# A perceiver block on one core: ScalarE takes over one layer's normalisation, and the projections behind it change their order

## The chip, the cores and the metric

The kernel runs on one core of one Trainium2 chip. The metric is the device time of one execution in microseconds (us), as the median of three runs of the kernel before.

## The reference

Inputs are `x` (8 batches of 128 rows, 512 wide) and a context (8 batches of 2048 rows, 384 wide). Three residual layers follow one another:

```
x = x + cross_attention(layernorm(x), context)   # 8 heads of 64, softmax over the 2048 context rows, then @ Wo + bo
n = layernorm(x)
x = x + n + read(n)                              # q, k, v = n @ W + b; causal logits q k^T per batch;
                                                 # softmax over the QUERY axis, / sqrt(512), times v
x = x + ffn(layernorm(x))                        # 512 -> 2048 -> 512, relu, values rounded to small float formats
```

`layernorm` subtracts the row mean and divides by sqrt(variance + 1e-5).

## The kernel before, in words

One program holds an instruction list for each engine, written out by hand; engines meet on counted semaphores alone, and each engine takes its own list strictly in the order written. A float32 operand of a large product is split into a high and a low f16 part, and `three_passes` (line 370) makes high*high + low*high + high*low: 12 matmuls of 128x512 for one projection tile.

**The long first part** (to about 750 us of the span) is the cross attention: 128 slots of `steady(s)` on every engine. TensorE works several slots behind in its later steps, so a tail of five more calls of `steady` (slots SLOTS to SLOTS+4) follows it.

**The seam** is what this change touches. It leads from the cross attention to the second layer:
- TensorE (lines 606 to 625) makes the output projections `project_out(r)` of the eight 128-row groups r, the first seven between the last calls of `steady`. Then come `turn(1, r)`, four float32 transposes of group r of the normalised rows `o_all` into one of two PSUM banks (`v_ps`, `k_ps`, alternating), and `project(i)`, the q, k and v products of the second layer. They go into four banks `t_bank` (`e_ps`). Products 0 to 11 read rows of groups 0 to 3 (the first half), products 12 to 23 the second half; before, each half has its four q tiles first, then k, then v.
- ScalarE (lines 857 to 871) writes the high part of each transposed group (`turned_high`, line 824) and empties the q and k banks (`q_or_k`, line 830).
- VectorE (from line 1122) adds each projection to `x` (`residual`, line 1050), takes the row moments (`row_moments`, lines 1037 to 1042), normalises (`norm`, line 1044, reads `xr`, writes `o_all`), writes the low part of each transposed group (`turned_low`, line 1030) and empties the v banks (`v_rows`, line 1059). In the tail it also still accumulates the cross attention (`accumulate`, line 952).
- GpSimd (from line 1272) adds the bias row to `x` (`add_bias`), finishes the last stages of the cross attention (`p_low`, `o_norm`), and turns each variance into 1/sqrt (`inverse_deviation`, lines 1262 to 1265, which calls `inverse_root`: one addition at line 1200, one power at line 1202). Its order there is: add_bias 0, p_low, add_bias 1, p_low, o_norm, add_bias 2, inverse_deviation 0, then add_bias 3, 4, 5 each followed by inverse_deviation 1, 2, 3, then o_norm of the last stage, add_bias 6, inverse_deviation 4, add_bias 7, inverse_deviation 5, 6, 7, and then `add_norm` of all eight groups (line 1267).
- SyncE issues the transposing DMAs that feed `project_out`, the last pair after the last `o_norm`; ScalarE issued the loads of `xr` and of the weights earlier.

The order of TensorE at the seam, before, is this (lines 610 to 619):

```
turn(1, 0)
turn(1, 1)
turn(1, 2)
turn(1, 3)
project_out(7)
for i in range(4):
    turn(1, 4 + i)
    project(i)
for i in range(4, 13):
    project(i)
```

`turn(1, 2)` and every later one waits until VectorE has taken the low part of the group two before (`tr_split`), because the two PSUM banks alternate. A `project` of the first half waits for the low parts of groups 0 to 3.

**Behind the seam** come the per-batch logits, softmax and reads of the second layer, woven into the products of the second half, and then the feed-forward layer, which TensorE also fills.

Of the kernel before, what the change touches and what calls it, by code (L numbers as in the profile page):

```python
# [4 lines left out]
F32 = mybir.dt.float32  # L5
# [7 lines left out]
P = 128  # L13
# [41 lines left out]
def perceiver_kernel(nc, x, ctx_t, xwq, xwk, xwv, xwo, xbo, awq, abq, awk, abk, awv, abv,  # L55
# [11 lines left out]
        ("o_f", [P, 2, DH], F32),  # L67
# [56 lines left out]
     q_max, bias, low, fade, acc, o_rec, o_sum, o_f) = keep.values()  # L124
# [23 lines left out]
    with ExitStack() as ctx:  # L148
# [78 lines left out]
        ln_step = sem("ln_step")  # L227
        xn2_ready = sem("xn2_ready")
# [56 lines left out]
        def turn_at(what, r):  # L285
            return turns.index((what, r))

# [81 lines left out]
        def _(pe):  # L369
# [136 lines left out]
            def turn(what, r):  # L506

                at = turn_at(what, r)
                pe.wait_ge(xn2_ready, at + 1)
# [31 lines left out]
            def project(i):  # L541

                half, what, t = i // 12, i % 12 // 4, i % 4
                pe.wait_ge(wx_split, 4 * what + 8)
                pe.wait_ge(tr_split, turn_at(1, 4 * half + 3) + 1)

                if i < 4:
                    pe.wait_ge(x1_ready, (3, 4, 7, 8)[i])
                else:
                    copied_a, copied_v = 8 * ((i - 4) // 12) + min((i - 4) % 12 + 1, 8), 4 * ((i - 4) // 12) + (i - 4) % 12 - 7  # L550
                    if (i - 4) % 12 < 8:
                        pe.wait_ge(mm2_copied_a, copied_a)
                    else:
                        pe.wait_ge(mm2_copied_v, copied_v)
                acc = t_bank[i % 4]
# [55 lines left out]
            turn(1, 1)  # L611
            turn(1, 2)
            turn(1, 3)
            project_out(7)
            for i in range(4):
                turn(1, 4 + i)
                project(i)
            for i in range(4, 13):
                project(i)
# [42 lines left out]
        def _(act):  # L662
# [166 lines left out]

            def q_or_k(i):  # L830
                half, what, t = i // 12, i % 12 // 4, i % 4
                act.wait_ge(mm2_filled, i + 1)
                dst, col = ((q2, bq_col), (k2, bk_col))[what]
                act.activation(dst[:, t, half * 512:half * 512 + 512], t_bank[i % 4], ACT.Identity,
                               bias=col[:, t:t + 1], scale=1.0 / W_SCALE).then_inc(mm2_copied_a, 1)
# [21 lines left out]
            for r in range(5):  # L857
                turned_high(1, r)
            act.wait_ge(small_landed, 96)
            for i in range(4):  # L860
                q_or_k(i)
                if i < 3:
                    turned_high(1, 5 + i)
            for i in range(4, 8):
                q_or_k(i)
# [21 lines left out]
        def _(dve):  # L887
# [156 lines left out]
            def norm(i):  # L1044
                r = i % B
                dve.wait_ge(rstd_ready, len(x_groups) + i + 1)
# [12 lines left out]
            def v_rows(i):  # L1059
                half, t = i // 12, i % 4  # L1060
# [62 lines left out]
            for s in range(SLOTS + 1, SLOTS + PV_LAG + 1):  # L1123
                steady(s)
                residual(s - SLOTS - 1)
                if s > SLOTS + 1:
                    norm(s - SLOTS - 2)
            residual(5)
            norm(4)
            turned_low(1, 0)  # L1130
            turned_low(1, 1)
            residual(6)
            norm(5)
            turned_low(1, 2)
            norm(6)
            turned_low(1, 3)
            turned_low(1, 4)
            residual(7)
            norm(7)
            for r in range(5, B):  # L1140
                turned_low(1, r)
            dve.wait_ge(small_landed, 96)

# [3 lines left out]
            for i in range(8, 12):  # L1147
                v_rows(i)
                w1_high(0, i - 8)
            for b in range(4):  # L1150
                mask_logits(b)
                prob_norm(b)
                if b >= 1:
                    add_read(b - 1)
                    norm(B + b - 1)
            add_read(3)
            norm(B + 3)
# [6 lines left out]
            for b in range(5, B):  # L1164
# [4 lines left out]
                norm(B + b - 1)  # L1169
            add_read(7)  # L1170
            norm(B + 7)
# [13 lines left out]
        def _(pool):  # L1185
# [76 lines left out]
            def inverse_deviation(i):  # L1262
                r = i % B
                pool.wait_ge(var_ready, i + 1)
                inverse_root(mean_var[:, r, 1:2], rstd[:, r:r + 1], exponent[:, 0:1], len(x_groups) + i)

            def add_norm(r):

                pool.wait_ge(xn2_ready, r + 1)
# [55 lines left out]
```

## Time and profile before

| what | us |
|---|---|
| median of 3 runs | 982.43 |
| lowest and highest run | 982.3, 982.64 |
| the profiled execution, its own time | 983.69 |
| its span in the trace | 981.9 |
| TensorE (matmul) busy | 949.6 |
| VectorE, ScalarE, GpSimd busy | 565.5, 583.7, 463.9 |

The span is the part of the execution that the trace covers; the execution's own time has 1.8 us around it. Times within the trace count from the start of the span. In the rows, PE is TensorE's matmuls, PEld its weight loads, DVE is VectorE, ACT ScalarE, POOL GpSimd, and PEclk is the granted clock of TensorE as a share of 2.4 GHz.

### The profile page before, as it was taken

The numbers are of one execution on the slowest core, as the hardware profiler recorded it, in microseconds if no ns is written. First come the engines' busy times: TensorE is split into PE (matmuls) and PEld (weight loads), VectorE is DVE, ScalarE is ACT, GpSimd is POOL, SyncE is SP. The second block draws the span as 40 slices with busy tenths as digits, with TensorE's granted clock in tenths as the row PEclk, the third lists the DMA queues.
The fourth block names the chain that finished last, engine by engine and source line by source line (L and its number), as shares of the span: only waits on it lengthen the run. The fifth ranks groups of instructions, "written<-read, shape, count | busy, mean of one in ns | idle before, by whom it ended". The sixth has DMA issues, their size and how long they took to land.

```text
span 981.9 us, 19435 instructions
## 1 busy us (share of the span) xinstructions
PE 949.6 (97%) x7437; PEld 579.3 (59%) x7440; DVE 565.5 (58%) x1016; ACT 583.7 (59%) x1095; POOL 463.9 (47%) x355
## 2 busy tenths in 40 slices
PE   4789999999999999999999999999999899999998
PEld 2356666666666666666666666666665445544443
DVE  6535656565656565555555555557777735565533
ACT  3357777777777777777777777776666121222220
POOL 3245555666555556665555566655456640000000
PEclk9899999999999999999999999999999899999999
DMA  8138666766777676666676668659778301013311
GB/s 289 65 87 160 136 129 130 140 130 124 137 157 133 138 141 129 130 138 126 154 141 140 130 130 135 135 95 185 160 153 172 65 1 43 1 44 97 97 33 75
DMA packets 304491, 117.95 MB, mean 120 GB/s; under 512 B 281232, under 2 KB 281232, under 8 KB 304400
## 3 DMA queue, kind: packets, MB, share of 16 engines
q1 hardware_dynamic: 289968, 88.92, 46.6%
q10 hardware_dynamic: 14432, 27.79, 9.9%
q8 instruction: 61, 1.00, 0.4%
q14 instruction: 30, 0.25, 0.1%
HBM read 45.36 MB, written 2.10 MB: 48 GB/s over the span
## 4 chain that ended last, share of the span: by engine, by line
PE 90%; DVE 4%; POOL 2%; DMA 1%; issue 1%; ACT 1%; SPq 0%; ACTq 0%; POOLq 0%; DVEq 0%
PE v_ps L375 28%; PE k_ps L375 26%; PE e_ps L375 14%; PE e_ps L416 10%; PE o_ps L436 6%; PE o_ps L439 3%; PE o_ps L603 3%; DMA wq_raw<-in_xwq 1%; PE v_ps L576 1%; DVE x_in L899 0%; DMA raw<-in_ctx_t 0%; DVE stats L1040 0%; PE k_ps L520 0%; POOL p_l L1220 0%; POOL rstd L1202 0%
## 5 line engine op out<-in xcount | busy, mean ns | idle before, releaser
L1220 POOL TENSOR_TENSOR p_l<-p_f,p_h 128x1024 f16<-128x1024 f32 x128 | 278.0, 2172 | 278.8 <-ACT p_f L744 274.0
L940 DVE TENSOR_TENSOR k_l<-k_ps,k_h 128x512 f16<-128x512 f32 x128 | 88.5, 692 | 154.7 <-ACT k_h L716 154.7
L744 ACT ACTIVATE p_f<-e_ps,bias 128x512 f32<-128x512 f32 x256 | 176.8, 691 | 0.0
L742 ACT ACTIVATE p_h<-e_ps,bias 128x512 f16<-128x512 f32 x256 | 174.6, 682 | 0.1
L945 DVE TENSOR_REDUCE q_max<-e_ps 128x2 f32<-128x1024 f32 x128 | 156.6, 1223 | 14.4
L932 DVE TENSOR_TENSOR v<-v_ps,v 128x512 f16<-128x512 f32 x128 | 88.8, 694 | 113.4 <-ACT v L708 113.3
L375 PE MATMUL v_ps<-wv_h,ctx_h 128*128 128x256 f16 x768 | 127.3, 275 | 4.7 <-DVE v L932 3.3
L375 PE MATMUL v_ps<-wv_l,ctx_h 128*128 128x256 f16 x768 | 126.4, 274 | 0.0
L375 PE MATMUL v_ps<-wv_h,ctx_l 128*128 128x256 f16 x768 | 126.1, 273 | 0.0
L1212 POOL TENSOR_TENSOR ctx_l<-raw,ctx_h 128x1536 f16<-128x1536 f32 x32 | 99.2, 3099 | 28.8 <-ACT ctx_h L697 28.8
L708 ACT ACTIVATE v<-v_ps 128x512 f16<-128x512 f32 x128 | 76.2, 595 | 51.3 <-PE v_ps L375 51.0
L436 PE MATMUL o_ps<-v,pt_h 128*128 128x130 f16 x1024 | 106.2, 220 | 0.1
L375 PE MATMUL k_ps<-ctx_h,wk_h 128*128 128x512 f16 x384 | 104.2, 380 | 0.0
L375 PE MATMUL k_ps<-ctx_h,wk_l 128*128 128x512 f16 x384 | 103.8, 379 | 0.0
L375 PE MATMUL k_ps<-ctx_l,wk_h 128*128 128x512 f16 x384 | 103.8, 379 | 0.0
L375 PEld LDWEIGHTS v_ps<-wv_h,ctx_h 128*128 128x128 f16 x768 | 64.9, 98 | 65.0 <-issue 56.8
L439 PE MATMUL o_ps<-v,pt_l 128*128 128x65 f16 x1024 | 102.8, 192 | 0.0
L436 PEld LDWEIGHTS o_ps<-v,pt_h 128*128 128x128 f16 x1024 | 91.9, 97 | 15.8 <-issue 1.0
L439 PEld LDWEIGHTS o_ps<-v,pt_l 128*128 128x128 f16 x1024 | 90.4, 98 | 14.9
L722 ACT ACTIVATE bias<-q_max 128x2 f32<-128x2 f32 x128 | 26.3, 206 | 108.8 <-DVE q_max L945 105.9
L716 ACT ACTIVATE k_h<-k_ps 128x512 f16<-128x512 f32 x128 | 76.5, 597 | 24.4 <-PE k_ps L375 23.8
L375 PEld LDWEIGHTS v_ps<-wv_l,ctx_h 128*128 128x128 f16 x768 | 75.4, 98 | 8.9
(163 smaller groups left out, 1255.3 us busy)
## 6 DMA issues: line engine op xcount, KB each, us to landing
raw<-in_ctx_t ACTq DMA_DIRECT2D x26, 768.0 KB, 5.6
w_raw<-in_w_t SPq DMA_DIRECT2D x32, 256.0 KB, 2.8
raw<-in_ctx_t SPq DMA_DIRECT2D x6, 768.0 KB, 4.7
pt_h<-p_h SPq DMA_TRANSPOSE x128, 3.2
pt_l<-p_l SPq DMA_TRANSPOSE x128, 3.4
xr<-in_x ACTq DMA_DIRECT2D x8, 256.0 KB, 3.5
out<-xr SPq DMA_DIRECT2D x8, 256.0 KB, 2.0
x_in<-in_x SPq DMA_DIRECT2D x4, 256.0 KB, 5.2
```

The costliest lines, as they stand in the source:

```text
L375: mm = pe.matmul(acc, a(c), m(c), start=(i == 0), stop=(i == len(todo) - 1))
L416: mm = pe.matmul(e_ps[s % 2][:, h, :], left[rows, p, tokens], right[rows, n % 2, cols], start=first, stop=last)
L436: pe.matmul(acc_bank[:, h * VW:h * VW + VW], pt_h[:, s % T_RING, h * JT + j, :], v[g][:, tile, 2 * (p % 2) + h, :], start=(j == 0 and h == ...
L439: mm = pe.matmul(acc_bank[:, h * VW:h * VW + DH + 1], pt_l[:, s % T_RING, h * JT + j, :], v[g][:, tile, 2 * (p % 2) + h, 0:DH + 1], start= ...
L716: act.activation(k_h[:, n % 2, q * QW:q * QW + QW], k_ps[:, :], ACT.Copy).then_inc(k_hi, 1)
L742: act.activation(p_h[:, s % H_RING, h, :], e_ps[s % 2][:, h, :], ACT.Exp, scale=EXP_SCALE, bias=bias[:, n % 2, h, q:q + 1]).then_inc(p_hi, 1)
L744: act.activation(p_f[:, s % F_RING, h, :], e_ps[s % 2][:, h, :], ACT.Exp, scale=EXP_SCALE, bias=bias[:, n % 2, h, q:q + 1]).then_inc(p_ful ...
L932: dve.tensor_tensor(v[g][:, j0:j0 + 2, :, DH + 1:2 * DH + 1], v_ps[:, :].rearrange("p (j h d) -> p j h d", j=2, d=DH), v[g][:, j0:j0 + 2, ...
L940: dve.tensor_tensor(k_l[:, n % 2, cols], k_ps[:, :], k_h[:, n % 2, cols], ALU.subtract).then_inc(k_split, 1)
L945: dve.tensor_reduce(q_max[:, s % 2, :], e_ps[s % 2][:, :, :], AX, ALU.max, negate=True).then_inc(e_maxed, 1)
L1212: pool.tensor_tensor(ctx_l[b % 2][:, q, :, :], raw[:, i % 2, :, :], ctx_h[b % 2][:, q, :, :], ALU.subtract).then_inc(ctx_split, 1)
L1220: pool.tensor_tensor(p_l[:, s % L_RING, :, :], p_f[:, s % F_RING, :, :], p_h[:, s % H_RING, :, :], ALU.subtract).then_inc(p_split, 1)
```

## The change

ScalarE makes the first normalisation of the second layer, as `rstd * x + nshift`, in place of VectorE. GpSimd makes `nshift = -mean * rstd` with one more instruction of 128x1 after each of its eight powers. On TensorE the four value products of the first half come ahead of the q and k products, and each stands right behind the transpose that it needs (a value product reads one group of rows only); the table `products` now says which product is the k-th, and `project(k)` of the first four waits for its own group alone. VectorE empties the value banks between its low parts, and loses the eight normalisations, so its residual additions no longer stand behind them. The normalisation ahead of the third layer stays on VectorE.

```diff
--- before.py
+++ after.py
@@ -64,7 +64,7 @@
         ("stats", [P, B, 6], F32), ("mean_var", [P, B, 2], F32), ("rstd", [P, B], F32), ("exponent", [P, B], F32),
         ("q_max", [P, 2, 2], F32), ("bias", [P, 2, 2, QUARTERS], F32), ("low", [P, 2, 2, 1], F32),
         ("fade", [P, 2, 2, QUARTERS], F32), ("acc", [P, 2, 2, VW], F32), ("o_rec", [P, 2, 1], F32), ("o_sum", [P, 2, DH], F32),
-        ("o_f", [P, 2, DH], F32),
+        ("o_f", [P, 2, DH], F32), ("nshift", [P, B], F32),
     ])
 
     waiting, _ = place(nc, base0, [("o_half", [P, B, 2, D], F16)])
@@ -121,7 +121,7 @@
     assert ffn2_end <= ctx1_base
 
     (o_all, ident, causal, bo_row, bv_row, b2_row, bq_col, bk_col, b1_col, b2_half, stats, mean_var, rstd, exponent,
-     q_max, bias, low, fade, acc, o_rec, o_sum, o_f) = keep.values()
+     q_max, bias, low, fade, acc, o_rec, o_sum, o_f, nshift) = keep.values()
     q_h, q_l = queries.values()
     ctx_h, ctx_l = [even["ctx_h0"], odd["ctx_h1"]], [even["ctx_l0"], odd["ctx_l1"]]
     p_f, p_h, p_l, pt_h, pt_l = probs.values()
@@ -225,6 +225,8 @@
         acc_filled = sem("acc_filled")
         x1_ready = sem("x1_ready")
         ln_step = sem("ln_step")
+        nshift_ready = sem("nshift_ready")
+        xn1_ready = sem("xn1_ready")
         xn2_ready = sem("xn2_ready")
         x1n_ready = sem("x1n_ready")
         mm2_filled = sem("mm2_filled")
@@ -285,6 +287,15 @@
         def turn_at(what, r):
             return turns.index((what, r))
 
+
+
+        products = [(2, 0, t) for t in range(4)] + [(what, 0, t) for what in range(2) for t in range(4)] + \
+            [(what, 1, t) for what in range(3) for t in range(4)]
+
+        def copied_of(k):
+            by_act = sum(what < 2 for what, _, _ in products[:k + 1])
+            return by_act, k + 1 - by_act
+
         def turn_bank(what, r):
 
             return kv_bank[1 if what == 2 and r < 4 else turn_at(what, r) % 2]
@@ -506,7 +517,10 @@
             def turn(what, r):
 
                 at = turn_at(what, r)
-                pe.wait_ge(xn2_ready, at + 1)
+                if what == 1:
+                    pe.wait_ge(xn1_ready, r + 1)
+                else:
+                    pe.wait_ge(xn2_ready, r + 1)
 
                 if at < 2:
                     pe.wait_ge(x1_ready, 5 + at)
@@ -538,21 +552,19 @@
                 three_passes(out_bank(r), (lambda c: ot_h[:, c, rows], lambda c: ot_l[:, c, rows]),
                              (lambda c: w_h[0][:, c, :], lambda c: w_l[0][:, c, :]), DCH).then_inc(acc_filled, 1)
 
-            def project(i):
-
-                half, what, t = i // 12, i % 12 // 4, i % 4
+            def project(k):
+
+                what, half, t = products[k]
                 pe.wait_ge(wx_split, 4 * what + 8)
-                pe.wait_ge(tr_split, turn_at(1, 4 * half + 3) + 1)
-
-                if i < 4:
-                    pe.wait_ge(x1_ready, (3, 4, 7, 8)[i])
+                pe.wait_ge(tr_split, turn_at(1, k if k < 4 else 4 * half + 3) + 1)
+
+                if k < 4:
+                    pe.wait_ge(x1_ready, (3, 4, 7, 8)[k])
+                elif products[k - 4][0] < 2:
+                    pe.wait_ge(mm2_copied_a, copied_of(k - 4)[0])
                 else:
-                    copied_a, copied_v = 8 * ((i - 4) // 12) + min((i - 4) % 12 + 1, 8), 4 * ((i - 4) // 12) + (i - 4) % 12 - 7
-                    if (i - 4) % 12 < 8:
-                        pe.wait_ge(mm2_copied_a, copied_a)
-                    else:
-                        pe.wait_ge(mm2_copied_v, copied_v)
-                acc = t_bank[i % 4]
+                    pe.wait_ge(mm2_copied_v, copied_of(k - 4)[1])
+                acc = t_bank[k % 4]
                 if what < 2:
                     cols, rows = slice(t * P, t * P + P), slice(half * 512, half * 512 + 512)
                     mm = three_passes(acc, (lambda c: w_h[1 + what][:, c, cols], lambda c: w_l[1 + what][:, c, cols]),
@@ -609,13 +621,18 @@
                     project_out(r)
             turn(1, 0)
             turn(1, 1)
+            project(0)
             turn(1, 2)
+            project(1)
+            project_out(7)
             turn(1, 3)
-            project_out(7)
-            for i in range(4):
-                turn(1, 4 + i)
-                project(i)
-            for i in range(4, 13):
+            project(2)
+            turn(1, 4)
+            project(3)
+            for i in range(3):
+                turn(1, 5 + i)
+                project(4 + i)
+            for i in range(7, 13):
                 project(i)
             logits(0)
             for i in range(13, 16):
@@ -827,8 +844,13 @@
                 act.activation(at_h[:, :, r * P:r * P + P], turn_bank(what, r)[:, :].rearrange("p (c n) -> p c n", c=DCH),
                                ACT.Copy).then_inc(tr_hi, 1)
 
+            def norm(r):
+                act.wait_ge(nshift_ready, r + 1)
+                act.activation(o_all[:, r, :], xr[:, r, :], ACT.Identity, scale=rstd[:, r:r + 1], bias=nshift[:, r:r + 1])\
+                    .then_inc(xn1_ready, 1)
+
             def q_or_k(i):
-                half, what, t = i // 12, i % 12 // 4, i % 4
+                what, half, t = products[i]
                 act.wait_ge(mm2_filled, i + 1)
                 dst, col = ((q2, bq_col), (k2, bk_col))[what]
                 act.activation(dst[:, t, half * 512:half * 512 + 512], t_bank[i % 4], ACT.Identity,
@@ -855,13 +877,16 @@
             for s in range(SLOTS, SLOTS + X_LAG):
                 steady(s)
             for r in range(5):
+                norm(r)
+            for r in range(3):
                 turned_high(1, r)
+                norm(5 + r)
+            turned_high(1, 3)
+            turned_high(1, 4)
             act.wait_ge(small_landed, 96)
-            for i in range(4):
-                q_or_k(i)
-                if i < 3:
-                    turned_high(1, 5 + i)
-            for i in range(4, 8):
+            for i in range(4, 12):
+                if i < 7:
+                    turned_high(1, 1 + i)
                 q_or_k(i)
             for i in range(12, 16):
                 q_or_k(i)
@@ -1041,9 +1066,8 @@
                 dve.wait_ge(ln_step, i + 1)
                 dve.bn_aggr(mean_var[:, r, :], stats[:, r, :]).then_inc(var_ready, 1)
 
-            def norm(i):
-                r = i % B
-                dve.wait_ge(rstd_ready, len(x_groups) + i + 1)
+            def norm(r):
+                dve.wait_ge(rstd_ready, len(x_groups) + B + r + 1)
                 dve.tensor_scalar(o_all[:, r, :], xr[:, r, :], mean_var[:, r, 0:1], rstd[:, r:r + 1],
                                   ALU.subtract, ALU.mult).then_inc(xn2_ready, 1)
 
@@ -1057,7 +1081,7 @@
                 row_moments(r)
 
             def v_rows(i):
-                half, t = i // 12, i % 4
+                _, half, t = products[i]
                 dve.wait_ge(mm2_filled, i + 1)
                 dve.scalar_tensor_tensor(v2[:, 4 * half + t, :], t_bank[i % 4], 1.0 / W_SCALE, bv_row[:, :],
                                          ALU.mult, ALU.add).then_inc(mm2_copied_v, 1)
@@ -1123,38 +1147,31 @@
             for s in range(SLOTS + 1, SLOTS + PV_LAG + 1):
                 steady(s)
                 residual(s - SLOTS - 1)
-                if s > SLOTS + 1:
-                    norm(s - SLOTS - 2)
             residual(5)
-            norm(4)
             turned_low(1, 0)
+            residual(6)
             turned_low(1, 1)
-            residual(6)
-            norm(5)
             turned_low(1, 2)
-            norm(6)
-            turned_low(1, 3)
-            turned_low(1, 4)
             residual(7)
-            norm(7)
-            for r in range(5, B):
-                turned_low(1, r)
             dve.wait_ge(small_landed, 96)
+            for i in range(4):
+                turned_low(1, 3 + i)
+                v_rows(i)
+            turned_low(1, 7)
 
             dve.tensor_copy(b2_half[:, :], b2_row[:, :]).then_inc(b2_f16, 1)
             dve.wait_ge(b2_f16, 1)
             dve.tensor_copy(b2_row[:, :], b2_half[:, :]).then_inc(b2_ready, 1)
-            for i in range(8, 12):
-                v_rows(i)
-                w1_high(0, i - 8)
+            for j in range(4):
+                w1_high(0, j)
             for b in range(4):
                 mask_logits(b)
                 prob_norm(b)
                 if b >= 1:
                     add_read(b - 1)
-                    norm(B + b - 1)
+                    norm(b - 1)
             add_read(3)
-            norm(B + 3)
+            norm(3)
             for r in range(3):
                 turned_low(2, r)
             v_rows(20)
@@ -1166,9 +1183,9 @@
                 mask_logits(b)
                 prob_norm(b)
                 add_read(b - 1)
-                norm(B + b - 1)
+                norm(b - 1)
             add_read(7)
-            norm(B + 7)
+            norm(7)
 
             for block in range(BLOCKS):
                 hidden_block(block, block < BLOCKS - 1)
@@ -1263,10 +1280,14 @@
                 r = i % B
                 pool.wait_ge(var_ready, i + 1)
                 inverse_root(mean_var[:, r, 1:2], rstd[:, r:r + 1], exponent[:, 0:1], len(x_groups) + i)
+                if i < B:
+                    pool.wait_ge(rstd_ready, len(x_groups) + i + 1)
+                    pool.tensor_scalar(nshift[:, r:r + 1], mean_var[:, r, 0:1], rstd[:, r:r + 1], -1.0, ALU.mult, ALU.mult)\
+                        .then_inc(nshift_ready, 1)
 
             def add_norm(r):
 
-                pool.wait_ge(xn2_ready, r + 1)
+                pool.wait_ge(xn1_ready, r + 1)
                 pool.tensor_tensor(xr[:, r, :], xr[:, r, :], o_all[:, r, :], ALU.add).then_inc(x1n_ready, 1)
 
             pool.wait_ge(small_landed, 96)
```

## Rows read from the trace of the kernel before

**Rows 1.** The page: the chain that ended last, share of the span by engine.
```profile
PE 90%; DVE 4%; POOL 2%; DMA 1%; issue 1%; ACT 1%; SPq 0%; ACTq 0%; POOLq 0%; DVEq 0%
```

**Rows 2.** Waits of TensorE from 745 us on: total, times, longest.
```profile
PE v_ps L520 <- DVE at_l L1034: 4.1, 2, 2.8
PE k_ps L520 <- DVE xr L1054: 1.4, 1, 1.4
```

**Rows 3.** Timeline of TensorE at the seam: start, length, line, instructions, [idle before].
```profile
771.97 0.60 PE L520 MATMUL v_ps<-ident,o_all 128*128 128x128 f32 x4
774.01 0.63 PE L520 MATMUL k_ps<-ident,o_all 128*128 128x128 f32 x4 [1.44 <-DVE xr L1054]
777.48 1.09 PE L520 MATMUL v_ps<-ident,o_all 128*128 128x128 f32 x4 [2.85 <-DVE at_l L1034]
...
779.21 1.91 PE L375 MATMUL e_ps<-wo_h,q_h 128*128 128x512 f16 x4
...
796.03 1.03 PE L375 MATMUL e_ps<-at_h,ak_h 128*128 128x512 f16 x4
```

**Rows 4.** The chain of waits at the seam, in order of time.
```profile
784.09 0.44 PE v_ps L520 x4
784.53 2.59 PE e_ps L375 x12
```

**Rows 5.** One-microsecond stretches: busy PE, PEld, DVE, ACT, POOL; PEclk; DMA, GB/s.
```profile
776.00:777.00 1.00, 0.00 (x0) 0.00 (x0) 1.00 (x2) 0.00 (x0) 0.92 (x3) 0.84 0.37 53
...
783.00:784.00 1.00, 1.00 (x5) 0.48 (x4) 0.00 (x0) 0.00 (x0) 0.00 (x0) 0.75 0.00 0
...
25.00:26.00 1.00, 0.00 (x0) 0.00 (x0) 1.00 (x1) 0.00 (x0) 0.98 (x1) 0.87 0.00 0
...
32.00:33.00 1.00, 1.00 (x5) 0.43 (x4) 0.00 (x0) 0.00 (x0) 0.00 (x0) 0.71 0.00 0
...
48.00:49.00 1.00, 0.00 (x0) 0.00 (x0) 0.48 (x1) 0.48 (x1) 0.00 (x0) 1.00 0.00 0
```

**Rows 6.** Timeline of GpSimd at the seam.
```profile
763.34 0.58 POOL L1202 TENSOR_TENSOR rstd<-rstd,exponent 128x1 f32<-128x1 f32 x1
...
767.58 0.42 POOL L1200 TENSOR_SCALAR rstd<-mean_var 128x1 f32<-128x1 f32 x1 [0.16 <-DVE mean_var L1042]
...
770.08 0.42 POOL L1200 TENSOR_SCALAR rstd<-mean_var 128x1 f32<-128x1 f32 x1 [0.19 <-DVE mean_var L1042]
...
772.94 1.45 POOL L1260 TENSOR_TENSOR xr<-xr,bo_row 128x512 f32<-128x512 f32 x1
...
774.66 0.57 POOL L1202 TENSOR_TENSOR rstd<-rstd,exponent 128x1 f32<-128x1 f32 x1
...
787.52 0.22 POOL L1200 TENSOR_SCALAR rstd<-mean_var 128x1 f32<-128x1 f32 x1 [6.90 <-DVE mean_var L1042]
787.82 0.57 POOL L1202 TENSOR_TENSOR rstd<-rstd,exponent 128x1 f32<-128x1 f32 x1
```

**Rows 7.** Timeline of VectorE at the seam.
```profile
763.95 1.48 DVE L1047 TENSOR_SCALAR o_all<-xr,mean_var,rstd 128x512 f32<-128x512 f32 x1 [4.16 <-POOL rstd L1202]
...
776.66 0.68 DVE L1034 TENSOR_TENSOR at_l<-v_ps,at_h 128x512 f16<-128x512 f32 x1
...
785.80 0.68 DVE L1054 SCALAR_TENSOR_TENSOR xr<-e_ps,xr 128x512 f32<-128x512 f32 x1
786.52 0.69 DVE L1040 BATCH_NORM_STATS2 stats<-xr 128x6 f32<-128x512 f32 x1
787.25 0.18 DVE L1042 BATCH_NORM_AGGREGATE mean_var<-stats 128x2 f32<-128x6 f32 x1
```

**Rows 8.** Timeline of ScalarE at the seam.
```profile
772.60 0.60 ACT L827 ACTIVATE at_h<-v_ps 128x512 f16<-128x512 f32 x1 [15.08 <-PE v_ps L520]
...
787.22 0.69 ACT L834 ACTIVATE q<-e_ps,bq_col 128x512 f32<-128x512 f32 x1 [2.05 <-PE e_ps L375]
787.80 0.59 ACT L827 ACTIVATE at_h<-k_ps 128x512 f16<-128x512 f32 x1
```

## The prediction, made blind

> **What bounds the kernel now.** I read the page's chain first: TensorE holds 90% of it [rows 1]. From 745 us to the end TensorE waits for other engines only three times, twice for VectorE's low part `at_l` (4.1 us together) and once for a residual addition (1.4 us) [rows 2]. So the change is worth what it does to those waits and to TensorE's clock. TensorE's timeline at the seam shows 1.44 us ahead of `turn(1, 1)` and 2.85 us ahead of `turn(1, 2)` [rows 3]. The clock, in one-microsecond stretches, falls to half (1.2 GHz) inside the stretch at 776 us, after TensorE had done a single turn in over 4 us [rows 3], and is back inside the one at 783 us [rows 5].
>
> The whole loss: from `turn(1, 0)` at 771.97 to product 4 at 796.03 is 24.06 us [rows 3]. In it lie eight turns at 0.44 and five products of 12 matmuls at 2.59 [rows 4], 3.5 + 12.95 = 16.5 us at full clock. Lost: 7.6 us. No change here can gain more.
>
> Who set it? VectorE sat idle 4.16 us at `norm(0)` and then took 1.48 us for it [rows 7], but the chain that held TensorE at 777.48 is another: GpSimd's addition for group 6 at 772.94, its power for group 4, ready at 774.66 + 0.57 = 775.23 [rows 6], `norm(4)` on VectorE, and then the first low part, 776.66 to 777.34 [rows 7]; TensorE starts 0.14 later [rows 3]. VectorE took the low part of group 0 behind `norm(4)` because its list says so.
>
> **The change, part by part.**
>
> *The order on ScalarE.* Its new list reads `norm` 0 to 4, then `turned_high(1, 0)`. The first high part therefore still stands behind the fifth normalisation, and so behind GpSimd's fifth root, as before the low part did; the queue is another, the releaser is the same. The first product now needs that high part. GpSimd's order is untouched.
>
> *Four more GpSimd instructions ahead of the fifth root, and a fifth behind it.* The trace has no such instruction. The nearest is line 1200, also a `tensor_scalar` of 128x1: 0.22 us at 787.52 and 0.42 us at 767.58, beside a busy VectorE [rows 6]; the wait for one's own result adds 0.08 (787.52 + 0.22 against 787.82) [rows 6]. So 0.30 to 0.50 each; I take 0.40. Four: +1.6 (1.2 to 2.0). A gain is excluded, since it is added work in one list. The two waits of 0.16 and 0.19 for row moments [rows 6] go, as VectorE no longer stops at `norm`: -0.35. The addition of 1.45 us may get up to 0.2 shorter without `norm` beside it; I count -0.1. The fifth root comes at 775.23 + 1.6 - 0.35 - 0.1 = 776.4, its shift at 776.8 (776.2 to 777.3).
>
> *From there to TensorE.* ScalarE has no normalisation from SBUF in this trace; the nearest is line 834, float32 with a bias column, 0.69 us, with the next instruction 0.58 after its start [rows 8]. Bounds: 0.5, the 0.60 of a high part less its overlap with the next, and 0.9, should the source cost more. I take 0.6, the nearest row; then 0.60 for the high part, 0.68 for the low part, 0.03 at the hand-over as from 772.57 to 772.60 [rows 3, 8] and 0.14 into TensorE [rows 3, 7]: 0.6 + 0.60 + 0.68 + 0.03 + 0.14 = 2.05, and 776.8 + 2.05 = 778.85. Since I left the addition's gain small, I take 778.7 for the first value product (778.1 to 779.5). Before, TensorE went on at 777.48. The idle stretch runs from the end of `turn(1, 1)`, now at 772.8, unbroken: about 5.9 us.
>
> *The clock.* Before, it fell during a stretch with one turn in it; now the stretch is empty, so I expect the fall at the same place. It came back at 783.7. At the kernel's start it fell at about 25.9 and came back at about 32.7 [rows 5]: both low stretches are 6.8 us long. I take 783.7 again. The product from 778.7 then runs at half rate, 5.0 us of clock for 2.5 us of work: it ends at 783.75. Before, two turns and `project_out(7)` paid this price, from 777.48 on.
> The Trainium skill (TensorE: Matmul & The Clock Gate, "What's actually happening") has the slow state as the default that activity lifts, at a point that isn't tied to the kernel's own work. By that rule the return need not stay at 783.7 in the new kernel; the trace, with two equal low stretches, neither shows nor denies it. What an earlier or no low stretch would give is rival 1.
>
> *The rest in order.* `turn(1, 2)` and product 1 to 786.8 (group 1's high part waits for `norm(5)`, whose shift comes one addition, one root and one shift after the fifth: from 772.94 to 775.23 it was 2.3 us without the shift [rows 6], so at 779.5, and the low part by 781.5: covered by product 0). `project_out(7)` to 789.4. `turn(1, 3)`, product 2, `turn(1, 4)`: 0.44 + 2.59 + 0.44 = 3.47 us. Then product 3 needs the low part of group 3. In ScalarE's list that high part stands behind `norm(7)`, which hangs on `project_out(7)` through the whole chain: 0.25 from TensorE to VectorE (0.1 from the chain's end of a product, 784.53 + 2.59, to ScalarE's start at 787.22 [rows 4, 8], and 0.16 because work in the timeline ends that much after the next has started, 0.60 against 0.44 for a turn [rows 3, 4]), addition and moments 785.80 to 787.43 = 1.63 [rows 7], 0.09 to GpSimd, root 0.87 [rows 6], shift 0.30, `norm(7)` 0.6, high, low and hand-overs 1.45. Sum 5.2 us against 3.47 of cover: **a new wait of 1.7 us**. Product 3 runs from 794.6 to 797.2. With the three turns that are still to come (1.3 us) the eight turns and five products are done at 798.5, where before they were at 796.03: **+2.45 us**.
>
> *What costs nothing.* The value products only change places, so TensorE's work is the same 16.5 us. VectorE's four `v_rows` move ahead, beside products 4 to 7, and leave VectorE free later, where it does not end any wait. `accumulate` and `residual` come up to 4 us earlier; this lets TensorE arrive some 0.2 us sooner at a stretch where it waits anyway. `turn(1, 1)` no longer waits: 1.44 us, which only lengthens the wait behind it. Shifts 5 and 6 lie under product 0. The last `o_norm` and SyncE's two transposing DMAs come about 1.2 us later; `project_out(7)` moved 7.6 us later, so they are covered; were they not, it would be up to 1.2 us. SyncE's weight loads behind them are for work 30 us later. `add_norm` starts some 4 us later on GpSimd; its reader, the addition of the first read, is more than ten products away.
>
> **The sum.** +2.45, of which some 0.1 is my rounding: +2.4. Against the profiled execution: span 981.9 + 2.4 = 984.3, its own time 983.69 + 2.4 = 986.1. That execution stands 1.3 us above the median of the runs, so for the median I forecast 982.43 + 2.4 = **984.8 us**. Own range of this case: restart of the product 778.1 to 779.5 is worth only half of itself while the clock is low (-0.3 to +0.6), `norm` at 0.5 to 0.9 once more in the later wait (-0.1 to +0.3), so 984.3 to 985.8. A measurement of this kernel can tell about 0.2% (2.0 us) from no change.
>
> **The rivals.**
> 1. *The clock is kinder (ends not slower).* At full clock product 0 takes 2.59 instead of 5.0 us: -2.4, giving 982.4; with the cheap GpSimd prices besides, 981.8. It decides where the clock is back by about 781. If it came back at 781, the gain is half of that, giving 983.5. For: the delay from resumed work to full clock is known from one case here, 777.48 to 783.7 [rows 3, 5], and nothing shows it to be fixed. Against: both falls came with no more idleness than the new one has, and both low stretches are equally long [rows 5]. The skill's rule named above leaves it open. Chance 0.13.
> 2. *ScalarE isn't held by `norm(4)` (the change does what it is built for).* If the first high part followed `turn(1, 0)` at once, product 0 would start at 772.6 + 0.6 + 0.7 + 0.14 = 774.0 and the clock would stay; product 1 would end at 779.6, `project_out(7)` at 782.2, and the later wait would still come: all done at 791.3, -4.7: 977.7. It needs GpSimd's fifth root before 771; it came at 775.23 [rows 6], and nothing in GpSimd's list was moved ahead. Chance 0.06.
> 3. *GpSimd's shifts are dear.* At 0.8 us each instead of 0.4 four of them and the fifth move the restart by 2.0, to 780.7. If the clock still returns at 783.7, half of it counts: 985.8; if it returns 2 us later too, all of it: 986.8. For: 128x1 operations there have cost twice as much beside VectorE [rows 6]. Chance 0.13.
> 4. *The new wait of 1.7 us costs the clock again.* A low stretch of 6.8 us loses 3.4: 988.2. Against: an empty microsecond at 48 us and the 1.44 us at 772 left the clock full [rows 3, 5]. Chance 0.06.
>
> The forecast keeps 0.62. Range: its own 984.3 to 985.8, rival 3 up to 986.8, and half of rival 1, down to 982.5; left out are rival 2, rival 4 and the ends of 1 and 3. Faster by over 0.2%: rival 2 and the far end of rival 1, 0.08. Within 0.2%: the rest of rival 1 and that part of the forecast's case that lies below 984.4: 0.28. Slower: 0.64.
>
> **What the new profile should show.** TensorE idle once, for 5 to 7 us between `turn(1, 1)` and the first value product, released by `at_l`; ScalarE idle ahead of the fifth normalisation, released by GpSimd; `nshift` at 0.2 to 0.45 us; the clock at half from about 776.8 to 783.7; a second wait of about 1.7 us ahead of the fourth value product, whose chain leads back to `project_out(7)`; product 4 of the list at about 797.7 and no other wait changed. Wrong if the clock stays full, if the first high part stands ahead of `norm(4)` in time, or if product 3 follows `turn(1, 4)` at once.

## The result, and the profile after

The changed kernel takes 985.42 us (median of 9 runs, 984.72 to 987.24) against 982.52 us (9 runs, 981.88 to 983.56) for the kernel before: 2.9 us slower, ratio 1.003 with a 95% interval of 1.0019 to 1.0040. The forecast was 984.8 us. The profiled execution took 985.47 us, its span is 983.3 us.

The timeline of TensorE at the seam, changed kernel, answers to [rows 3]; line 534 is a turn, line 386 a product or output projection:

```profile
771.16 0.60 PE L534 MATMUL v_ps<-ident,o_all 128*128 128x128 f32 x4
771.59 0.60 PE L534 MATMUL k_ps<-ident,o_all 128*128 128x128 f32 x4
777.84 1.86 PE L386 MATMUL e_ps<-av_h,at_h 128*128 128x512 f16 x4 [5.64 <-issue]
...
782.68 0.60 PE L534 MATMUL v_ps<-ident,o_all 128*128 128x128 f32 x4
...
788.30 0.60 PE L534 MATMUL k_ps<-ident,o_all 128*128 128x128 f32 x4
...
791.33 0.60 PE L534 MATMUL v_ps<-ident,o_all 128*128 128x128 f32 x4
793.69 1.02 PE L386 MATMUL e_ps<-av_h,at_h 128*128 128x512 f16 x4 [1.76 <-issue]
...
796.71 1.03 PE L386 MATMUL e_ps<-at_h,aq_h 128*128 128x512 f16 x4
```

There is one wait of 5.64 us ahead of the first value product and a second of 1.76 us ahead of the fourth. The page of the profile puts both down to "issue": it found no releaser for them. VectorE's timeline shows who it was, the low parts `at_l` of group 0 and of group 3, each ending 0.1 us before the product:

```profile
777.04 0.69 DVE L1059 TENSOR_TENSOR at_l<-v_ps,at_h 128x512 f16<-128x512 f32 x1 [5.21 <-ACT at_h L844]
...
788.50 0.69 DVE L1078 SCALAR_TENSOR_TENSOR xr<-e_ps,xr 128x512 f32<-128x512 f32 x1 [3.86 <-PE e_ps L386]
...
792.90 0.69 DVE L1059 TENSOR_TENSOR at_l<-k_ps,at_h 128x512 f16<-128x512 f32 x1 [2.76 <-ACT at_h L844]
```

Both point on to ScalarE. Its timeline (line 849 is the normalisation, 844 a high part) answers to [rows 8]:

```profile
771.45 0.81 ACT L849 ACTIVATE o_all<-xr,nshift,rstd 128x512 f32<-128x512 f32 x1 [1.74 <-POOL nshift L1285]
775.72 0.81 ACT L849 ACTIVATE o_all<-xr,nshift,rstd 128x512 f32<-128x512 f32 x1 [3.45 <-POOL nshift L1285]
776.44 0.57 ACT L844 ACTIVATE at_h<-v_ps 128x512 f16<-128x512 f32 x1
...
791.50 0.81 ACT L849 ACTIVATE o_all<-xr,nshift,rstd 128x512 f32<-128x512 f32 x1 [7.58 <-POOL nshift L1285]
792.22 0.58 ACT L844 ACTIVATE at_h<-k_ps 128x512 f16<-128x512 f32 x1
```

Group 0 had been turned at 771.76, but its high part starts at 776.44, straight behind the fifth normalisation; group 3 had been turned at 788.90, and its high part starts at 792.22, straight behind the eighth. ScalarE idled through all of the 3.45 us with group 0's high part ready to be taken, and through the last 2.6 of the 7.58 us with group 3's. What the fifth normalisation waited for is GpSimd, to be read against [rows 6]:

```profile
773.09 1.26 POOL L1277 TENSOR_TENSOR xr<-xr,bo_row 128x512 f32<-128x512 f32 x1
774.44 0.22 POOL L1217 TENSOR_SCALAR rstd<-mean_var 128x1 f32<-128x1 f32 x1
774.74 0.57 POOL L1219 TENSOR_TENSOR rstd<-rstd,exponent 128x1 f32<-128x1 f32 x1
775.41 0.27 POOL L1285 TENSOR_SCALAR nshift<-mean_var,rstd 128x1 f32<-128x1 f32 x1
```

The clock, in one-microsecond stretches (the column ahead of the last two is PEclk), against [rows 5]:

```profile
775.00:776.00 1.00, 0.00 (x0) 0.00 (x0) 0.00 (x0) 0.28 (x1) 0.90 (x3) 0.81 0.36 73
...
782.00:783.00 1.00, 1.00 (x6) 0.60 (x5) 0.00 (x0) 0.00 (x0) 0.00 (x0) 0.78 0.00 0
```

It is at half from about 775.6 to 782.4, and the first value product takes 4.84 us (777.84 to 782.68) where the second takes 2.59.

**Where the time went.** Call the seam the time from the first turn to the point at which eight turns and five products are done. Before it was 24.06 us [rows 3]. After, product 4 starts at 796.71 with two turns (0.44 each) still to come: 796.71 + 0.87 - 771.16 = 26.42 us, +2.36. TensorE reached the seam 0.81 us sooner, and a later wait is 0.14 us shorter (1.28 against 1.14), so the two spans differ by 2.36 - 0.81 - 0.14 = 1.4 us, as they do (983.3 against 981.9). The 0.81 us can't be put down to the change: `before_again` below, unedited, arrives 0.65 us sooner too. The two executions differ by 1.8 us (985.47 against 983.69), because the changed kernel spends 2.2 us outside the span where the kernel before spends 1.8. The medians differ by 2.9, because the profiled execution of before stood 1.2 us above its own median.

### The profile page after: what moved, and what is told of

Same layout as the page of the kernel before. It is cut to its first block, busy times and chain, and to the rows that moved or that the text cites. A ratio compares the mean times of both kernels' runs of the same rounds, so it can differ in the third digit from the quotient of the medians.

```text
span 983.3 us, 19447 instructions
## 1 busy us (share of the span) xinstructions
PE 946.8 (96%) x7440; PEld 578.2 (59%) x7440; DVE 557.4 (57%) x1008; ACT 590.5 (60%) x1103; POOL 464.8 (47%) x363
## 4 chain that ended last, share of the span: by engine, by line
PE 92%; DVE 3%; DMA 1%; issue 1%; POOL 1%; ACT 1%; SPq 0%; POOLq 0%
PE v_ps L386 28%; PE k_ps L386 26%; PE e_ps L386 15%; PE e_ps L427 10%; PE o_ps L447 6%; PE o_ps L450 3%; PE o_ps L615 3%; DMA wq_raw<-in_xwq 1%; PE v_ps L588 1%; DVE x_in L924 0%; DMA raw<-in_ctx_t 0%; PE k_ps L534 0%; PE o_ps L596 0%; POOL ctx_l L1229 0%; ACT ctx_h L714 0%
## 5 line engine op out<-in xcount | busy, mean ns | idle before, releaser
L386 PEld LDWEIGHTS v_ps<-wv_h,ctx_l 128*128 128x128 f16 x768 | 75.5, 98 | 9.0
```

Source lines behind the costliest of these rows:

```text
L386: mm = pe.matmul(acc, a(c), m(c), start=(i == 0), stop=(i == len(todo) - 1))
```

## The experiments

The theory: ScalarE's list holds the high part of group 0 behind the fifth normalisation, and that of group 3 behind the eighth. The rivals: GpSimd's shifts, the order of products in itself, the clock alone. All times are medians, set against runs of the kernel before on the same chip; the seams are read from the profile of each kernel as above (`turn_early` has one output projection inside, 2.59 us, taken off). A distance to the changed kernel is that between two medians from different lots of runs, whose medians of before differ by up to 0.4 us (982.52 to 982.88).

| kernel | us | us before | ratio (95%) | seam, us | waits in it, us |
|---|---|---|---|---|---|
| changed | 985.42 | 982.52 | 1.0019 to 1.0040 | 26.42 | 5.64, 1.76 |
| high_first | 979.82 | 982.79 | 0.9955 to 0.9980 | 20.19 | 1.49, 1.76 |
| fourth_high | 984.84 | 982.79 | 1.0006 to 1.0024 | 24.66 | 5.40 |
| both_high | 977.59 | 982.79 | 0.9928 to 0.9955 | 17.92 | 1.14 |
| kept_busy | 983.80 | 982.79 | 1.0001 to 1.0018 | 24.20 | 0.51, 1.76 |
| norm_only | 984.02 | 982.74 | 1.0002 to 1.0020 | 24.98 | 5.43 |
| order_only | 984.35 | 982.74 | 1.0008 to 1.0026 | 25.42 | 1.43, 2.80, 1.39 |
| double_shift | 988.47 | 982.74 | 1.0045 to 1.0070 | 29.24 | 0.23, 6.89, 2.12 |
| before_low_first | 980.12 | 982.74 | 0.9962 to 0.9983 | 20.40 | 1.43, 0.89, 0.62 |
| turn_early | 975.58 | 982.88 | 0.9909 to 0.9936 | 16.44 | none |

**1. high_first**

```diff
-            for r in range(5):
-                norm(r)
-            for r in range(3):
-                turned_high(1, r)
-                norm(5 + r)
+            norm(0)
+            norm(1)
+            norm(2)
+            norm(3)
+            turned_high(1, 0)
+            turned_high(1, 1)
+            norm(4)
+            norm(5)
+            norm(6)
+            turned_high(1, 2)
+            norm(7)
```

> The changed kernel with one edit: in ScalarE's list the high parts of groups 0 and 1 stand ahead of the fifth normalisation, the high part of group 3 stays behind the eighth. Theory (the order of ScalarE's list holds the first product): the wait ahead of the first value product shrinks from 5.6 us to about 1.6 us, released by at_l at 773.5, the clock stays full, the second wait of 1.8 us stays; about 6 us under the changed kernel, 979.4 us. Rival (the clock falls anyway, or group 1's low part becomes the bound): only 2 to 4 us under it, 981.5 to 983.5. Rival (GpSimd's shifts are the loss): no change, 985.4.

979.82 us. TensorE's timeline, to be read against the first fence above:

```profile
773.44 0.60 PE L534 MATMUL k_ps<-ident,o_all 128*128 128x128 f32 x4
775.53 1.02 PE L386 MATMUL e_ps<-av_h,at_h 128*128 128x512 f16 x4 [1.49 <-issue]
...
789.30 1.02 PE L386 MATMUL e_ps<-av_h,at_h 128*128 128x512 f16 x4 [1.76 <-issue]
```

The first wait falls from 5.64 to 1.49 us, the first four matmuls take 1.02 us instead of 1.86 (full clock), and the second wait stays to the hundredth. (Another 0.18 us ahead of the second product, 778.73 - 778.11 against 0.44 for a turn, is in no row as a wait; `both_high` has it too.) The shifts and the product order are as in the changed kernel, so neither is the loss by itself. Two high parts moved ahead in one list are worth 5.6 us.

**2. fourth_high**: `turned_high(1, 3)` ahead of `norm(7)`, the first high part left behind `norm(4)`.

> The changed kernel with one edit: in ScalarE's list the high part of group 3 stands ahead of the eighth normalisation. Theory: the second wait of TensorE (1.8 us ahead of the fourth value product) goes, the first of 5.6 us stays with its half clock; 1.7 us under the changed kernel, 983.7 us. Rival: the wait only moves, to the turn of group 7 or to the product behind it, and the time stays at 985.4.

984.84 us, 0.6 us under the changed kernel, where 1.7 were expected. In the profile the second wait is gone and nothing took its place: the seam is 24.66, 1.76 us shorter. The rival of a moved wait falls. The profile also reaches the seam at 772.62 instead of 771.16, and it is just as late long before anything that was edited, as the first `k_h` behind 97 us shows (changed kernel, then this one):

```profile
97.20 0.60 ACT L733 ACTIVATE k_h<-k_ps 128x512 f16<-128x512 f32 x1 [0.19 <-PE k_ps L386]
```

```profile
98.66 0.60 ACT L733 ACTIVATE k_h<-k_ps 128x512 f16<-128x512 f32 x1 [0.19 <-PE k_ps L386]
```

Over the profiles of the changed kernel and its variants with nothing edited ahead of the seam, the arrival lies anywhere from 770.93 to 773.00; it belongs to the execution, not to the edit. The expected 983.7 us lies inside the interval (982.79 x 1.0006 is 983.4); the runs spread from 982.64 to 985.38. So the wait and its length are shown, and what it is worth in the median, 0.6 or 1.7 us, is not settled by this run.

**3. both_high**: both edits, and `turned_high(1, 2)` right behind `norm(5)`.

> The changed kernel with both edits of ScalarE's list: high parts of groups 0 and 1 ahead of the fifth normalisation, that of group 2 right behind the sixth, that of group 3 ahead of the eighth. Theory: one wait of about 1.6 us is left ahead of the first value product, at full clock; about 8 us under the changed kernel, 977.4 us, and 5 us under the kernel before. Rival (the gains overlap or VectorE becomes the bound, since its addition for group 6 stands ahead of group 1's low part): 979 to 981 us.

977.59 us, 7.8 us under the changed kernel and 5.2 under the one before. The two losses add up (6.23 + 1.76 = 7.99 against 8.50 in the seam; of the rest, 0.35 is the first wait, 1.14 us here and 1.49 in high_first).

**4. kept_busy**

```diff
             turn(1, 1)
+            pe.wait_ge(x1_ready, 3)
+            for i in range(24):
+                pe.matmul(t_bank[0], w_h[0][:, i % DCH, 0:P], w_h[0][:, i % DCH, :], start=True, stop=True)
             project(0)
```

> The changed kernel plus 24 matmuls of 128x512 whose result is overwritten, between the turn of group 1 and the first value product (about 5.2 us of work at full clock, inside the wait of 5.6 us). It prices the clock alone. Theory: the clock stays full, the first value product still starts at about 777.8 but takes 2.6 us in place of 4.8; 2.3 us under the changed kernel, 983.1 us. Rival (the clock is not lost to the idle stretch): no gain, 985.4, or slower where the extra matmuls delay the product.

983.80 us:

```profile
772.21 5.34 PE L626 MATMUL e_ps<-wo_h 128*128 128x512 f16 x24
778.06 1.02 PE L386 MATMUL e_ps<-av_h,at_h 128*128 128x512 f16 x4 [0.51 <-issue]
```

The product starts as far behind the second turn as in the changed kernel (6.29 against 6.25 us), but at full clock; the seam is 2.22 us shorter, the time 1.6 us. So of what the first wait costs, about two microseconds are clock and the rest is the wait itself. Useless matmuls pay here, though less than removing the wait.

**5. norm_only**: the changed kernel with the old order of TensorE and of the low parts.

> The first part of the change alone: ScalarE normalises with GpSimd's shift, while TensorE keeps the old order (four turns, the last output projection, then a turn and a q product each); in ScalarE's list the first high part stands behind the fifth normalisation, and the eighth comes after the high parts of groups 3 and 4. Theory (GpSimd's shifts delay the fifth root and the queue behind it holds the first high part): TensorE no longer waits ahead of the second turn but waits about 5.5 us ahead of the third, the clock falls for the same length, no second wait; 0 to 1 us over the kernel before, 983.3 us. Rival (the move to ScalarE is itself the loss of 2.9 us): 985.4. Rival (it is a gain, given back by the product order): under 982.

**6. order_only**: the changed kernel with the old normalisation on VectorE (its fifth ahead of the first low part, its eighth ahead of that of group 3) and no shifts.

> The other part alone: the new order of products, with VectorE still normalising, its fifth normalisation ahead of the first low part and its eighth ahead of that of group 3, no shifts on GpSimd. Theory: the first value product starts about when the third turn did before (5 us idle in two pieces, half clock), and the new order brings a second wait of about 0.8 us ahead of the fourth value product; 0.5 to 1.5 us over the kernel before, 983.8 us. Rival (the order is the whole loss): 985.4. Rival (the order is a gain): under 982.

984.02 and 984.35 us, +1.28 and +1.61 over the kernel before: together 2.89. Each interval is 1.8 us wide, so that the sum meets the 2.9 so closely is partly chance; that both parts lose is shown, as neither interval reaches 1. Each does so by its own mechanism. `norm_only` has one wait ahead of the third turn; `order_only` keeps the two old waits and adds the new one:

```profile
774.72 0.63 PE L531 MATMUL k_ps<-ident,o_all 128*128 128x128 f32 x4 [1.43 <-DVE xr L1074]
778.15 1.87 PE L386 MATMUL e_ps<-av_h,at_h 128*128 128x512 f16 x4 [2.80 <-issue]
...
794.22 1.02 PE L386 MATMUL e_ps<-av_h,at_h 128*128 128x512 f16 x4 [1.39 <-issue]
```

The new wait came out at 1.39 us where I had expected 0.8, since VectorE's eighth normalisation, started 0.06 us behind one of GpSimd's additions (`add_norm` at 791.97), took 1.48 us where the sixth took 0.52:

```profile
792.03 1.48 DVE L1067 TENSOR_SCALAR o_all<-xr,mean_var,rstd 128x512 f32<-128x512 f32 x1 [1.00 <-POOL rstd L1221]
```

**7. double_shift**

```diff
                         .then_inc(nshift_ready, 1)
+                    pool.wait_ge(nshift_ready, 2 * i + 1)
+                    pool.tensor_scalar(nshift[:, r:r + 1], mean_var[:, r, 0:1], rstd[:, r:r + 1], -1.0, ALU.mult, ALU.mult)\
+                        .then_inc(nshift_ready, 1)
```

> The changed kernel with every shift made twice on GpSimd, the second behind the first, and ScalarE waiting for both: it doubles the suspected cost. One shift costs about 0.36 us in GpSimd's list. Theory: the first value product comes 1.8 us later; while the clock is at half only a part of it counts, and the second wait grows by 0.36; 1.3 to 2.2 us over the changed kernel, 987.1 us. Rival (the shifts are covered): 985.4.

988.47 us, 3.0 over the changed kernel where 1.3 to 2.2 were expected. The product starts 8.34 us behind the first turn instead of 6.68, so one shift costs 1.66 / 5 = 0.33 us in GpSimd's list. The shifts lengthen the wait, then, and ScalarE's list is what lets it reach TensorE; the new normalisation without any shift was not run. The second wait grew by 0.36 to 2.12 us, and behind it the clock fell once more, which it had not done behind 1.76 us:

```profile
794.78 1.02 PE L386 MATMUL e_ps<-av_h,at_h 128*128 128x512 f16 x4 [2.12 <-issue]
795.65 1.62 PE L386 MATMUL e_ps<-av_h,at_l 128*128 128x512 f16 x4
797.07 1.91 PE L386 MATMUL e_ps<-av_l,at_h 128*128 128x512 f16 x4
```

```profile
795.00:796.00 1.00, 1.00 (x6) 0.48 (x5) 1.00 (x3) 0.00 (x0) 1.00 (x2) 0.97 0.00 0
...
799.00:800.00 1.00, 1.00 (x7) 0.75 (x6) 0.00 (x0) 0.25 (x1) 1.00 (x2) 0.83 0.00 0
```

Product 3 and the turn behind it took 799.49 - 794.78 = 4.71 us instead of 3.02, so this is 1.7 us of the result.

**8. before_low_first**, on the kernel before:

```diff
             residual(5)
-            norm(4)
             turned_low(1, 0)
             turned_low(1, 1)
+            norm(4)
             residual(6)
```

> The kernel before with one edit: in VectorE's list the low parts of groups 0 and 1 stand ahead of the fifth normalisation. Theory (the seam is set by which queue holds the first split part behind the fifth normalisation, in both kernels): the third turn starts at about 775.6 instead of 777.5, the clock stays full, a wait of 1 to 1.5 us remains ahead of the first product; 3 to 4 us under the kernel before, 979.4 us. Rival (the transposes of the last output or GpSimd's additions bound the seam anyway): 982 us or more.

980.12 us, 2.6 us faster than the kernel before with one entry moved, where 3 to 4 were expected. The third turn starts at 775.39, the clock stays full and the waits are 1.43, 0.89 and 0.62. (The seam is 3.7 us shorter than in the first profile of before, and 2.1 shorter than in the second below.) The kernel before had the same defect in VectorE's list that the changed one has in ScalarE's.

**9. turn_early**

```diff
                 for r in ((0, 1), (2,), (3,), (4,), (5, 6))[s - SLOTS]:
+                    if r == 6:
+                        turn(1, 0)
                     project_out(r)
-            turn(1, 0)
             turn(1, 1)
...
+            turned_low(1, 0)
             residual(5)
-            turned_low(1, 0)
+            turned_low(1, 1)
             residual(6)
-            turned_low(1, 1)
             turned_low(1, 2)
```

with ScalarE's list as norm 0, 1, 2, high 0, norm 3, high 1, norm 4, 5, high 2, norm 6, high 3, norm 7, high 4.

> Both edits of ScalarE's list, and besides: TensorE turns group 0 ahead of the output projection of group 6, ScalarE takes its high part ahead of the fourth normalisation, VectorE its low part ahead of the residual addition of group 5 (and that of group 1 ahead of the one of group 6). Theory: the last wait of 1.1 us ahead of the first value product goes, as does the 0.2 us ahead of the second; 1.3 us under both_high, 976.3 us. Rival (group 5's addition and so the turn of group 1 come late): 977.6 or more.

975.58 us, where 976.3 was expected: 0.8% under the kernel before (ratio 0.9922, 0.9909 to 0.9936) and the fastest here. TensorE runs through the seam:

```profile
771.43 0.60 PE L534 MATMUL k_ps<-ident,o_all 128*128 128x128 f32 x4
771.87 1.03 PE L386 MATMUL e_ps<-av_h,at_h 128*128 128x512 f16 x4
...
786.56 1.03 PE L386 MATMUL e_ps<-at_h,aq_h 128*128 128x512 f16 x4
```

786.56 + 0.87 - 768.40 (its first turn) - 2.59 = 16.44 us, the 16.5 us of pure work that the prediction had worked out. Nothing more is to be had at this seam without less work.

**10. before_again and 11. after_again**, unedited:

> The kernel before once more, for a second profile. It tells how much of the seam's 24.06 us (from the first turn to the point at which eight turns and five products are done) belongs to the place at which the clock falls and returns. Theory: 23 to 24.1 us, the two waits of 1.4 and 2.9 us unchanged, only the half-clock stretch moved.

> The changed kernel once more, for a second profile. Theory: the waits of 5.6 and 1.8 us unchanged; the seam 26.4 us, or up to 2 us off where the clock falls or returns at another point, or falls once more behind the second wait as it did in double_shift.

The changed kernel repeats itself (985.17 us, waits 5.62 and 1.76, seam 26.37). The kernel before does not (981.56 us): the same two waits, but the stretches of its second profile show the clock at half for 3.4 us only, from 776.3 to 779.7, instead of 6.8 us:

```profile
776.00:777.00 1.00, 0.16 (x1) 0.19 (x2) 1.00 (x3) 0.00 (x0) 0.74 (x2) 0.63 0.79 162
...
779.00:780.00 1.00, 1.00 (x5) 0.41 (x4) 0.86 (x2) 0.41 (x1) 0.89 (x2) 0.66 0.42 158
```

Its seam is 22.50 us against 24.06, below the 23 to 24.1 that were expected. The span is 2.2 us shorter: 1.56 at the seam and 0.65 ahead of it. So the kernel before has a spread of its own, and the pair of first profiles, 1.8 us apart, understates the loss; this second pair is 3.6 us apart.

## Why the prediction was right

- **The list of ScalarE as the holder.** Right, and shown by high_first: the high part stood behind the fifth normalisation, 5.6 us.
- **GpSimd's four shifts.** One was priced at 0.40 us; the instruction takes 0.27 us, and from a root's first instruction to the next addition it is 1.22 us in GpSimd's timeline (762.45 to 763.67) where it was 0.86 (763.02 to 763.88): 0.36 each, 0.33 by double_shift. Part of it was given back, which the prediction had at nothing: the first instruction of the second to fourth root fell from 0.40 to 0.42 us to 0.22 or 0.23. And the addition for group 6 took 1.26 us instead of 1.45, 0.2 less where 0.1 was counted. The fifth shift ended 4.5 us behind the first turn, where I had 4.8.
- **ScalarE's normalisation.** Sized too small: 0.81 us, the next instruction 0.72 behind its start, against 0.6. The nearest row [rows 8] reads PSUM and has a column for the bias only; this one reads SBUF and has columns for both. Which of these two makes the difference was not tried. The product started 6.68 us behind the first turn, forecast 6.73. That is closer than its parts: 0.3 us too much on GpSimd stood against 0.1 too little on ScalarE and against the 0.15 that the forecast had taken off (778.85 to 778.7) without a row for it.
- **The clock.** Half from about 775.6 to 782.4, 6.8 us, as taken from [rows 5]; the product took 4.84 us, forecast 5.0. (The shares 0.84 and 0.75 in [rows 5] put the stretch of before at 776.7 to 783.5; the 783.7 of the prediction is 0.2 late, worth 0.1 us.) The rule that the return isn't tied to the kernel's own work (Trainium skill, TensorE: Matmul & The Clock Gate, "What's actually happening") is borne out by before_again: 3.4 us in one execution, 6.8 in another, with the same waits. It changed the kernel before, not the changed one. The prediction argued that both low stretches of before were 6.8 us long and missed a third in the same trace, which lasts 3.4 us, from 66.7 to 70.1:

```profile
66.00:67.00 1.00, 0.94 (x8) 0.83 (x9) 0.13 (x1) 1.00 (x3) 1.00 (x1) 0.85 0.52 199
...
70.00:71.00 1.00, 1.00 (x6) 0.39 (x5) 0.69 (x1) 1.00 (x3) 0.19 (x1) 0.94 0.43 9
```

  So a short stretch was less of a guess than rival 1 made it. At the seam it stayed the exception: of the eight profiles whose clock fell ahead of the first product of the seam, seven show 6.8 us and one, before_again, 3.4.
- **The second wait.** 1.76 us of idleness, forecast 1.7; fourth_high removed it alone. The prediction counted from start to start, and so counted the wait is 1.92 us (793.69 - 791.33 - 0.44): 0.2 too little, of which 0.12 is the normalisation and 0.08 the shift.
- **The sum.** Seam +2.36 against +2.45 forecast, with two errors that cancel: the first product ended 11.5 us behind the first turn, not 11.8, and the second wait was 0.2 us longer. The time was +2.9, forecast +2.4. Of the missing 0.5 us, 0.3 lies outside the span: the prediction carried over the 1.8 us of before, but each of the nine executions of the changed kernel has 2.1 to 2.2 us there, each of the 53 of before beside the experiments 1.8 to 1.9. What causes it is open. The rest is in the reference: I set the change against one profiled execution of before and took its distance to the median (1.3 us) as one that both kernels share, but the changed kernel's stood 0.05 us above its median. Against the second profile of before the seam is 26.42 - 22.50 = 3.9 us longer. Which of the two stretches the median runs of before had is not on record, so how far the seam is longer in the median is not shown beyond these two, +2.4 and +3.9. The mechanism was right; that the time came within 0.6 us of 984.8 is in part luck.
- **The rivals.** The kind clock did not come; the dear shifts neither. The fourth, that the new wait costs the clock again, did not happen in either profile of the changed kernel, but did in double_shift at 2.12 us; whether it explains the one run of 987.24 us is open. The second rival, an unblocked ScalarE, was priced at 977.7 us with the second wait kept. The kernel that does this is high_first, and it took 979.82, 2.1 us more; its seam is 20.2 us where the price had 19.3. That both_high took 977.59 is chance, as it has no second wait.

## What to carry to other kernels

When work moves to an idle engine, read the place of every instruction in that engine's list, not its load: ScalarE was idle for 3.45 us with the instruction that TensorE needed next in its list. Put what another engine waits for ahead of what waits itself, and check the kernel at hand for the same fault before rebuilding it (one moved entry gained 2.6 us here, a rebuilt order lost 2.9, and the rebuilt order with its own queue put right gained 5.2). The wait of 5.6 us on TensorE cost its length and then about 2 us of half clock, and how much of the latter comes can differ between executions of one kernel (3.4 or 6.8 us at half), so a single profile of the reference is a reference with an error of its own.

## What was not expected of the hardware

The same kernel kept TensorE at half clock for 6.8 us in one execution and for 3.4 us in another, with equal waits of 1.44 and 2.85 us. A lone wait of 1.76 us left the clock full in all four profiles that have it (the two of the changed kernel, high_first, kept_busy), one of 2.12 us at the same place did not. The changed kernel spends 0.3 us more outside its span than the kernel before (2.2 against 1.8 us); order_only has 1.8 there and norm_only 2.0, and the cause is open. Two 128x512 float32 instructions on ScalarE differ by 0.12 us (0.81 against 0.69), as described above.
